# Score matmuls as row tiles of 32x128, one per subhead, in a differential attention kernel

## The reference

```python
q = (x @ Wq.T).reshape(b, t, 2 * H, D)          # H = 8, so 16 subheads, D = 8
k = (x @ Wk.T).reshape(b, t, 2 * H, D)
v = (x @ Wv.T).reshape(b, t, H, 2 * D)
q = _apply_rope(q, freqs, scale)
k = _apply_rope(k, freqs, 1.0 / scale)
scores = jnp.einsum('bhtd,bhsd->bhts', q, k)     # 1024 x 1024 for each of 2 x 16 subheads
probs = jax.nn.softmax(scores.astype(jnp.float32), axis=-1)
probs = probs.reshape(b, H, 2, t, t)
diff = probs[:, :, 0] - lam * probs[:, :, 1]
attn = jnp.einsum('bhts,bhsd->bhtd', diff, v)
```

## Time and profile before

| | us |
|---|---|
| median of 3 runs | 549.23 (548.25 to 549.42) |
| the profiled execution | 547.23 |
| its span in the trace | 545.4 |
| PE busy | 517.8 (95%) |
| DVE busy | 458.2 (84%) |
| ACT busy | 339.3 (62%) |
| mean granted clock of TensorE over the span | 0.981 |

### The profile page before, as it was taken

One profiled execution on the slowest core, in us unless ns is written; L12 is line 12 of the kernel. 1 busy time (PEld: TensorE's weight loads), 2 busy tenths in 40 slices (PEclk: granted clock), 3 DMA queues, 4 the chain that ended last, 5 costly groups with the idle time before them and its releaser, 6 DMA issues.

```text
span 545.4 us, 8613 instructions
## 1 busy us (share of the span) xinstructions
PE 517.8 (95%) x2607; PEld 295.6 (54%) x2607; DVE 458.2 (84%) x800; ACT 339.3 (62%) x424; POOL 68.8 (13%) x69
## 2 busy tenths in 40 slices
PE   6586999999999999999999999999999999999995
PEld 5564677777555554545555454555545455554333
DVE  2986778999889999999999999999999999998116
ACT  1440687666757666675766666666666666666872
POOL 3186961300000000000000000000000000000000
PEclk9697999999999999999999999999999999999999
DMA  9135526100000010020002001000200020000002
GB/s 314 53 108 199 176 100 199 55 1 2 0 2 1 13 58 2 1 70 0 1 1 67 1 0 46 23 1 0 69 1 0 2 67 3 0 2 1 2 2 77
DMA packets 11771, 23.46 MB, mean 43 GB/s; under 512 B 1490, under 2 KB 6226, under 8 KB 11618
## 3 DMA queue, kind: packets, MB, share of 16 engines
q1 hardware_dynamic: 11314, 20.34, 11.7%
q10 hardware_dynamic: 432, 2.81, 1.4%
HBM read 14.43 MB, written 8.39 MB: 42 GB/s over the span
## 4 chain that ended last, share of the span: by engine, by line
PE 74%; DVE 14%; DMA 4%; ACT 3%; issue 2%; POOL 1%; SPq 1%; ACTq 0%; DVEq 0%; POOLq 0%
PE ps L994 24%; PE ps L1023 23%; PE ps L1016 22%; DVE part_max L683 4%; DVE hL L722 4%; DMA X<-in_x 2%; ACT h L478 1%; PE ps L937 1%; DVE wbH L628 1%; DMA q_scr<-ropeL 1%; ACT hH L481 1%; DVE wbL L630 1%; DMA wb_raw<-in_wb 1%; PE ps L1010 1%; PE ps L862 1%
## 5 line engine op out<-in xcount | busy, mean ns | idle before, releaser
L683 DVE TENSOR_REDUCE part_max<-ps 128x1 f32<-128x512 f32 x512 | 340.1, 688 | 25.4 <-PE ps L994 22.3
L512 ACT ACTIVATE E<-ps 128x1024 f32<-128x1024 f32 x256 | 248.2, 1022 | 125.0 <-PE ps L1016 125.0
L994 PE MATMUL ps<-K,Q 128*128 128x512 f32 x512 | 193.7, 421 | 0.8 <-DVE part_max L683 0.3
L1016 PE MATMUL ps<-Q,K 128*128 128x512 f32 x512 | 161.4, 399 | 0.2 <-ACT zT L486 0.2
L994 PEld LDWEIGHTS ps<-K,Q 128*128 128x128 f32 x512 | 96.0, 188 | 119.3 <-DVE part_max L683 100.7
L1023 PE MATMUL ps<-E,Vg 128*32 128x512 f32 x1024 | 136.4, 605 | 0.6 <-ACT E L512 0.6
L1016 PEld LDWEIGHTS ps<-Q,K 128*128 128x128 f32 x512 | 94.8, 188 | 27.7 <-ACT E L512 10.3
L417 POOL TENSOR_TENSOR U<-AT,rsum 128x256 f32 (+1 forms) x15 | 9.3, 623 | 392.2 <-DVE rsum L776 392.2
L478 ACT ACTIVATE h<-ps 128x512 f32<-128x512 f32 x48 | 28.6, 595 | 38.0 <-PE ps L864 30.8
L722 DVE TENSOR_TENSOR hL<-h,hH 128x512 fp32r<-128x512 f32 x48 | 37.8, 802 | 8.0 <-ACT hH L481 8.0
L1023 PEld LDWEIGHTS ps<-E,Vg 128*32 128x32 f32 x1024 | 20.1, 108 | 44.7 <-issue 34.9
(11 more groups left out here) (140 smaller groups left out, 321.9 us busy)
## 6 DMA issues: line engine op xcount, KB each, us to landing
Q<-q_scr SPq DMA_DIRECT2D x8, 512.0 KB
K<-k_scr SPq DMA_DIRECT2D x32, 96.0 KB
tab<-in_tables ACTq DMA_DIRECT2D x1, 2048.0 KB, 11.4
q_scr<-ropeL SPq DMA_DIRECT2D x4, 512.0 KB, 5.7
q_scr<-ropeH SPq DMA_DIRECT2D x4, 512.0 KB, 4.6
k_scr<-ropeH SPq DMA_DIRECT2D x4, 512.0 KB, 5.1
wa_raw<-in_wa SPq DMA_DIRECT2D x6, 256.0 KB, 3.0
wb_raw<-in_wb SPq DMA_DIRECT2D x6, 256.0 KB, 3.6
```

The costliest lines, as they stand in the source:

```text
L512: nc.scalar.activation(E[:, par, 2 * jj:2 * jj + 2, :].rearrange("p j t -> p (j t)"), ps[:, 2 * jj:2 * jj + 2, :].rearrange("p j t -> p (j ...
L683: nc.vector.tensor_reduce(part_max[:, half, col, sh:sh + 1], ps[:, ring_bank(x), :], AX.X, ALU.max).then_inc(slot_read, 1)
L994: mm(ps[:, ring_bank(x + sh), :], Q[:, g % 2, k // GJ * P:(k // GJ + 1) * P], K[:, g % 2, k % GJ, sh * BANK:(sh + 1) * BANK], start=True, ...
L1016: last = mm(ps[:, j, :], K[:, par, j, st * P:(st + 1) * P], Q[:, par, th * BANK:(th + 1) * BANK], start=True, stop=True)
```

## The change

In `scores`, both operands are cut to the 32 partitions of subhead j. The matmuls thereby become row tiles of 32 rows by 128 columns, at row 32j of the array, where they were 128 by 128. Number, order, waits, results and banks of all instructions stay as they are, and the matmuls of `max_slot` still use all 128 rows.

```diff
             def scores(s, par, jj):
                 th, st = s // TB, s % TB
                 for j in (2 * jj, 2 * jj + 1):
-                    last = mm(ps[:, j, :], K[:, par, j, st * P:(st + 1) * P], Q[:, par, th * BANK:(th + 1) * BANK],
+                    rows = slice(QUAD * j, QUAD * (j + 1))
+                    last = mm(ps[:, j, :], K[rows, par, j, st * P:(st + 1) * P], Q[rows, par, th * BANK:(th + 1) * BANK],
                               start=True, stop=True)
                 last.then_inc(st_done, 1)
```

## The result

| | before | after |
|---|---|---|
| median of runs | 549.33 us (4 runs, 548.25 to 552.34) | 583.36 us (4 runs, 582.68 to 585.99) |
| ratio | | 1.0619 (95% interval 1.0566 to 1.0672) |
| the profiled execution | 547.23 | 583.43 |
| its span | 545.4 | 581.6 |

The change makes the kernel 6.2% slower, at 583.4 us against a forecast of 584.5.

What follows compares the result with a forecast made beforehand. PE was taken as the bound, 3.078 us a step, DVE 0.22 behind. Borders +0.80 and overlap -0.47 give +0.33 a step, +38.3 us over 116 steps; with -3 for the last 12 and 2.0 for the median, 584.5 us, range 555 to 615.

Steps and rivals of the forecast that it cites:

- Term 1: PE's order in a step with maxima: four added tile-size changes, into and out of each score pair, +0.80 us.
- Term 2: Score pairs in a step: the two matmuls of each pair run at once, -0.47 us a step.
- The choice between the ends: Score pairs: -0.47 us a step with full overlap or 0.00 with none; -0.47 was taken.
- serial loads: Rival in score pairs: weight loads go one after the other, saving only 0.25 a step; 610 us, chance 0.18.
- Terms 3 and 4: Score weight loads: no gain or loss, 0; other engines: ACT and DVE not in the way, PE stays the bound.
- Term 5: Last 12 steps, without maxima: no border added and pairs get shorter, gain between 0 and 4.7, taken as -3 us.
- A clock below 1.00 in the loop: Sign in the loop that the forecast is wrong: granted clock falls below 1.00, as holes make PE less active.
- 559: Rival at entries into score pairs: cheap entry, borders cost +0.58 a step instead of +0.80; 559 us, chance 0.17.
- 610: Rival in score pairs: the two weight loads go one after the other, +0.55 a step; 610 us, chance 0.18.
- 639: Rival in score pairs: no overlap at all, +0.80 us a step; 639 us, chance 0.08.
- The rival "faster": Score pairs: changing rows alone is no border, so DVE's 2.854 a step decides; 520 to 535 us, chance 0.07.

Runs made afterwards that it cites:

- two kernels that have only borders: Against the kernel before: only the loop's maxima as row tiles, 639.66 us; scores as 64-row tiles, both of a pair on the same rows, 639.21 us.
- The kernel without borders: The kernel after with the loop's maxima matmuls also as 32x128 row tiles: 510.07 us, ratio to before 0.9267; run again, 513.13 us.
- the first experiment: The kernel after with the loop's maxima matmuls also as 32x128 row tiles: 510.07 us median of 5, ratio to before 0.9267.

## Why the prediction was right

- **The bound.** PE set the step before and sets it after; DVE and ACT are busy as long as before and only wait more. Shown by the stage rows. L683's idle time grows by 35.8 us (24.8 to 60.6) and ACT's before L512 by 30.7, where 38 was said for both.
- **Term 1, four borders at 0.20.** Shown: 0.192 in each of two kernels that have only borders, 0.195 in the kernel after if a pair saves the full 0.235 ((0.31 + 0.47) / 4). The reading of two borders in one place each, and the earlier trace rows, held for row tiles of 32 and 64 rows and for both directions. The rows carried less than was read from them: in the earlier trace rows L862's load starts at 30.82, before the record of L901 ends at 30.89, so "once that is done" is not in them, and a record's end is modelled. The load of L1017 starts 0.43 after that of L994, not the 0.32 that was said; 0.32 is right from where the L994 begins to stream, 0.11 behind its record's start. L994 behind the pair has 0.49 to 0.50, as said.
- **Term 2, a pair as one.** Shown: 0.18 for both loads, and 52.6 us over 115 steps with and without the overlap. The choice between the ends, by L1023's fours, was the right one, and serial loads did not occur.
- **Terms 3 and 4.** Loads 0.181 against 0.188 us; ACT and DVE not in the way.
- **The sum.** 116 x 0.33 = 38.3 was put down, 116 x 0.31 = 36.0 measured; the 2 us are the third digit of the border. In its first part the forecast was right by its mechanism.
- **Term 5, -3 us.** Right at a clock of 1.00: 2.73 by the stage rows, 2.9 by the medians. In the profiled execution of the kernel after it was 0.65, since the granted clock was 0.87 in that stretch. A clock below 1.00 in the loop was named as a sign that the forecast would be wrong. It came, in these 12 steps alone, and cost 2.1 us (27.25 against 25.17).
- **Luck.** From profile to profile the span grew by 36.2 us, with 35.3 forecast: 2.3 too much for the 116 steps, 2.35 too much gain in the last 12, and 0.8 of scatter ahead of them. So small misses cancel. The 2.0 us added for the median over the profiled execution did not return either: the kernel after has a median of 583.36 and a profiled execution of 583.43. That 584.5 lies so near 583.4 is luck by some 2 us; that it lies near 583 and not near 559, 610 or 639 is not.
- **The rival "faster".** Its condition (borders under 0.12) was rightly called unlikely. Its price was wrong: "DVE's 2.854 can't be passed", so 520 at best. The kernel without borders took 509 to 510, with steps of 2.69. What was wrong in it is taking DVE's busy time as its floor. A reduction has a record of 0.68 to 0.69 us, but four back to back take 2.48, with starts 0.60 apart: records of neighbours overlap, as a matmul's do. In the kernel before PE delivers the maxima further apart, so the records overlap less and the busy time holds some of that spacing. The reductions were busy for 307.5 / 115 = 2.67 us a step there. At 4 x 0.60 = 2.40 the floor of a step would be about 2.854 - 0.27 = 2.58, an estimate. No run reaches it: the mean step without borders is 2.76, with DVE busy for 2.64 of it.

## What to carry to other kernels

Small matmuls as row tiles run together, but in this kernel every change of tile size between neighbours in PE's order costs nearly as much (0.19 us) as one 512-column matmul takes (0.235). So count the borders in the instruction order first, and if there are any to add, group the tiled matmuls or tile their neighbours as well. The busy time of an engine is no lower bound of its time when the records of its instructions overlap (DVE's 545 instructions were busy for 328 us before and for 303 without borders): take the length of a back-to-back run.

## What was unexpected in the hardware

- The border is the same, 0.192 us, for 32 rows and 64 rows.
- Row tiles on different rows overlap fully: four of 512 columns take the same 0.44 us to the next load as two. A matmul for the maxima starts with those of the scores too (301.63 in the first experiment).
- With only 32-row tiles beside the products, 7 of 18 executions (both kernels together) had a mean granted clock of 0.960 or less, the worst 0.767 and 17% longer. No execution of the other kernels had a mean below 0.97, though single stretches did (0.87 above). PE is idle for an eighth of the time in these two kernels and has fewer rows at work as well. Which of the two it is, or whether it is either, was not separated; it stays open.
